# Splitting the routed tokens of an attention and expert layer into parts of five and three batches, and moving twelve row normalisations from VectorE to ScalarE

## What is computed

```python
x = _layernorm(x + attention(x))               # 8 batches x 512 tokens x 256
# experts: 16 routed ones, 4 chosen per token (gate_w), width 128; one shared expert of width 256
c[token, expert] = score of the 4 chosen experts, else 0
y = sum over experts e of  c[t, e] * (silu(x @ w1[e]) * (x @ w3[e])) @ w2[e]
z = (silu(x @ ws1) * (x @ ws3)) @ ws2
x = _layernorm(x + y + z)
```

## Time and profile before

| | |
|---|---|
| time, three runs | 698.48, 701.73, 703.09 us; median 701.73 us |
| profiled execution | 698.33 us, of it 696.5 us from the first to the last instruction (the span) |
| PE busy | 517.0 us (74%) |
| DVE busy | 427.1 us (61%) |
| ACT busy | 300.6 us (43%) |
| POOL busy | 290.6 us (42%) |
| first and last start of a pair's L1036 | 274.3 and 583.2 us |
| granted TensorE clock, mean | 0.925 |

### The profile page before, as it was taken

How to read it: one execution, slowest core, us unless ns; L and a number is a source line. 1 busy time by engine, 2 the same in 40 slices (tenths; PEclk the granted TensorE clock), 3 DMA queues, 4 the chain that set the end, 5 groups by cost and what they waited for, 6 DMA issues and landing times.

```text
span 696.5 us, 13485 instructions
## 1 busy us (share of the span) xinstructions
PE 517.0 (74%) x3554; PEld 355.2 (51%) x3555; DVE 427.1 (61%) x1200; ACT 300.6 (43%) x659; POOL 290.6 (42%) x334
## 2 busy tenths in 40 slices
PE   1899886789897787888886787888887779782300
PEld 1355543455454356676674566676765666441100
DVE  2447783777755877557654344366757657585384
ACT  2536644446334252555554555355645446121000
POOL 1000126365455421545644200634435450787664
PEclk9999999799999989999999999899999999997555
DMA  7022338285561302677767776677777763334232
GB/s 193 25 76 77 124 118 288 75 274 192 202 225 54 113 31 69 220 231 241 252 243 247 252 226 210 189 232 226 222 246 230 240 198 137 99 120 123 83 113 98
DMA packets 64091, 118.63 MB, mean 170 GB/s; under 512 B 9760, under 2 KB 23088, under 8 KB 64048
## 3 DMA queue, kind: packets, MB, share of 16 engines
q1 hardware_dynamic: 51216, 84.55, 37.2%
q0 software_dynamic: 12288, 33.57, 15.4%
q10 hardware_dynamic: 544, 0.00, 0.0%
HBM read 55.17 MB, written 62.91 MB: 170 GB/s over the span
## 4 chain that ended last, share of the span: by engine, by line
PE 35%; issue 17%; DVE 17%; SPq 8%; POOL 7%; ACT 5%; DMA 5%; another core or an unknown queue 5%; DVEq 0%; ACTq 0%; POOLq 0%
PE t L1340 4%; PE h_even L1149 3%; PE h_even L1151 3%; PE h_even L1150 3%; PE h_odd L1149 3%; PE h_odd L1151 3%; PE h_odd L1150 3%; DMA kv<-expert_in 2%; PE y L1186 2%; SPq L327 2%; POOL q_fm L452 2%; SPq L330 2%; POOL wa_stage L452 2%; POOL gate L452 2%
## 5 line engine op out<-in xcount | busy, mean ns | idle before, releaser
L440 POOL DMA_INDIRECT expert_in<-x_all,slots x128 | 132.9, 1038 | 111.7 <-PE h_odd L1151 45.1
L1340 PE MATMUL t<-ident,kv 128*128 128x128 f32 x384 | 61.7, 283 | 23.8 <-DMA kv<-expert_in 16.6
L452 POOL DMA_INDIRECT wa_stage<-expert_out,result_of x64 | 62.9, 982 | 28.2 <-issue 17.5
L452 POOL DMA_INDIRECT q_fm<-expert_out,result_of x32 | 32.1, 1003 | 89.8 <-DMA expert_out<-q_exp 64.1
L1044 DVE TENSOR_TENSOR wa_lo<-bias_heads,wa_hi 128x256 bf16<-128x256 f32 x96 | 40.5, 422 | 46.6 <-ACT wa_hi L642 37.2
L426 POOL TENSOR_SCALAR neg_mean<-mv 128x4 f32<-128x4 f32 x16 | 4.6, 290 | 148.7 <-DVE mv L699 148.5
L1340 PEld LDWEIGHTS t<-ident,kv 128*128 128x128 f32 x384 | 44.9, 145 | 33.8 <-issue 17.6
L1025 DVE TENSOR_TENSOR xsT_lo<-t,xsT_hi 128x512 bf16<-128x512 f32 x72 | 49.4, 688 | 13.2 <-ACT xsT_hi L617 6.6
L1150 PE MATMUL h_even<-xsT_lo,we_hi 128*128 128x256 bf16 x192 | 53.6, 279 | 2.2 <-issue 2.2
L1149 PE MATMUL h_even<-xsT_hi,we_hi 128*128 128x256 f16 x192 | 53.5, 279 | 1.8 <-DVE bias_heads L1036 1.3
L1151 PE MATMUL h_even<-xsT_hi,we_lo 128*128 128x256 f16 x192 | 53.6, 279 | 1.2 <-issue 1.1
(11 more groups left out here) (222 smaller groups left out, 1522.0 us busy)
## 6 DMA issues: line engine op xcount, KB each, us to landing
kv<-expert_in SPq DMA_DIRECT2D x96, 256.0 KB
expert_out<-k_exp SPq DMA_DIRECT2D x48, 256.0 KB
expert_out<-q_exp SPq DMA_DIRECT2D x48, 256.0 KB
expert_in<-wa_stage SPq DMA_DIRECT2D x16, 512.0 KB
expert_in<-wa_stage SPq DMA_DIRECT2D x32, 256.0 KB
stage<-in_L_ffn_w SPq DMA_DIRECT2D x48, 128.0 KB
x_in<-in_L_attn_x SPq DMA_DIRECT2D x8, 512.0 KB
out<-gated SPq DMA_DIRECT2D x8, 512.0 KB
```

Of the source, the lines that this page charges most:

```text
L440: pool.indirect_dma_start(xs_dram[b // WB], bass.IndirectOffsetOnAxis(ap=slots[:, b, t, j:j + 1], axis=0), x_all[:, b, t, :], None).then_i ...
L452: pool.indirect_dma_start(y_got[i][:, j, :], None, ys_dram[w], bass.IndirectOffsetOnAxis(ap=result_of[:, b, t, j:j + 1], axis=0)).then_inc ...
L1340: last = pe.transpose(t_bank[r % 2][:, c * 2 * P + i * P:c * 2 * P + (i + 1) * P], xs[r][:, i, c * P:(c + 1) * P], ident[:, :])
```

## The change

Part 0 now has five batches (0 to 4) and 56 pairs, part 1 three batches (5 to 7) and 40 pairs; there are still 96 pairs. What follows from it and what goes with it:

- `SPREAD` is 4, not 3: POOL dispatches 16 times in each of the iterations 3 to 7, 80 in all, which is all of part 0. Beside the pairs of part 0 it dispatches 48 times, not 64, a tile every 4 pairs.
- Beside the 40 pairs of part 1 POOL gathers 20 tiles (80 indirect DMAs), not 16 beside 48. Tile k waits for pair 56 + 17k/9. DVE adds 18 of the 20 tiles in the pairs 6 to 39 of the part, the last two in the first two `shared_hidden` of the tail.
- ACT, not DVE, normalises batches 0 to 2, one tile in a pair, from pair 16, 23 and 31 of the part. `rstd_of` now waits, for the layer norms behind the first of them, until the norm ahead of it has been applied (`out_ready`).
- In the tail POOL gathers 12 tiles, not 16. The two `rstd_of` for batches 3 and 4 both stand behind the four gathers of batch 5. DVE keeps its order, with a tile's number four higher at each step; the statistics of batches 5 and 6 now stand in the loop over batches, and 8 sums fewer are left.
- `count_region` for part 0 moves from batch 5 to batch 6 of the attention. One scratch area of the plan moves to `q_exp`. The loops of ACT and DVE over the pairs of part 1 are written out; those of PE and SP stay loops.

```diff
-SPREAD = 3
+SPREAD = 4
...
-    WB = NB // WAVES
-    WT = WB * TT
+    BATCHES = (5, 3)
+    START = (0, BATCHES[0], NB)
...
+    TILES = [TT * n for n in BATCHES]
+    NPAIR = [n * TOP_K // 2 + E for n in TILES]
...
+    EARLY = 3
...
+    SUM_PAIRS = (6, 40)
+    SUMMED = 18
+    NORM_PAIR = (16, 23, 31)
...
@@ rstd_of
                 pool.tensor_tensor(var_eps[:, :], mv[:, :, 1], eps[:, :], ALU.add).then_inc(rstd_step, 1)
+                if ln > NB:
+                    pool.wait_ge(out_ready, ln - NB)
...
@@ gather
-                if 0 < k < WT:
-                    pool.wait_ge(h_ready, NPAIR + (3 * k if k < WT - TT else 3 * WT - 13 + 2 * (k - WT + TT)))
+                if w == 0 and k > 0:
+                    pool.wait_ge(h_ready, FIRST[1] + 17 * k // 9)
...
@@ POOL beside the pairs of part 0
-            for i in range(WT):
+            for i in range(TILES[1]):
                 if i > 0:
-                    pool.wait_ge(h_ready, 5 * i // 2)
+                    pool.wait_ge(h_ready, 4 * i)
...
@@ POOL, gathers of both parts
-                for b in range(WB * w, WB * (w + 1)):
+                for b in range(START[w], START[w + 1]):
                     for t in range(TT):
                         gather(TT * b + t)
-                        if b > 0 and t == (1 if w == 0 else TT - 1):
+                        if w == 0 and t == TT - 2 and 0 < b <= EARLY:
                             rstd_of(NB + b - 1)
+                    if w == 1:
+                        for ln in range(EARLY if b == START[1] else b - 1, b):
+                            rstd_of(NB + ln)
...
@@ ACT
+            def final_norm(b, t):
+                if t == 0:
+                    act.wait_ge(rstd_ready, NB + b + 1)
+                    if b > 0:
+                        act.wait_ge(out_stored, 16 * b)
+                last = act.activation(o_sb[:, t, :], x_all[:, b, t, :], ACT.Identity, bias=shift[:, t:t + 1],
+                                      scale=rstd[:, t:t + 1])
...
+            norms = {NORM_PAIR[b] + t: (b, t) for b in range(EARLY) for t in range(TT)}
+            for p in range(NPAIR[1]):
+                pair(FIRST[1] + p, p % RING, PAIR_GROUPS[0] + p // RING, p < NPAIR[1] - 2, norms.get(p))
...
@@ DVE, pairs of part 1
+            for i in range(SUMMED * TOP_K):
+                at = SUM_PAIRS[0] + i * (SUM_PAIRS[1] - SUM_PAIRS[0]) // (SUMMED * TOP_K)
+                sums[at].append((i // (TT * TOP_K), i // TOP_K % TT, i % TOP_K))
...
@@ DVE, tail
-            for n in range(WB, NB):
-                at = 2 * (n - WB)
+            for n in range(EARLY, NB):
+                at = SHARED * (n - EARLY)
...
-                if n < WB + 2:
+                    if n > EARLY + 1:
+                        whole_norm(n - 2)
                     whole_stats(n - 1)
-            whole_stats(WB + 1)
```

More of the change, by code:

```diff
@@ L353, in _ @@
             sp.wait_ge(rows_ready, 1)
-            for b in range(WB):
+            for b in range(BATCHES[0]):
                 sp.wait_ge(dispatched[b], 16 * TT * TOP_K)
@@ L364, in _ @@
             sp.wait_ge(fill_rows_ready, 2)
-            with sp.Fori(3, (last - 1) // 2) as q2:
+            with sp.Fori(3, 5) as q2:
                 group(0, 2 * q2 + 1, fill=E + 2 * RING * (q2 - 3))
                 group(0, 2 * q2 + 2, fill=E + 2 * RING * (q2 - 3) + RING)
+            for q in range(11, last):
+                group(0, q)
             sp.wait_ge(rows_ready, 2)
-            for b in range(WB, NB):
+            for b in range(BATCHES[0], NB):
                 sp.wait_ge(dispatched[b], 16 * TT * TOP_K)
@@ L383, in _ @@
                 group(1, 2 * q2)
-            group(1, 5)
             store_out(0)
-            for q in range(6, 9):
+            for q in range(5, 7):
                 group(1, q)
             store_out(1)
-            for q in range(9, last):
+            for q in range(7, last1):
                 group(1, q)
             for r in range(-3, RING):
-                store_ys(1, RING * last + r, r % RING)
-            with sp.Fori(WB - 2, NB) as b:
+                store_ys(1, RING * last1 + r, r % RING)
+            with sp.Fori(EARLY - 1, NB) as b:
                 store_out(b)
@@ L625, in ys_copy, with pair @@
                                ACT.Copy).then_inc(ys_copied, 1)
-            def pair(g, r, group, ahead=True):
+            def final_norm(b, t):
[5 more added lines that the diff above has]
+                                      scale=rstd[:, t:t + 1])
+                if t == TT - 1:
+                    last.then_inc(out_ready, 1)
+            def pair(g, r, group, ahead=True, norm=None):
                 if ahead:
@@ L642, in pair, with group @@
                 act.activation(aT_hi[r % 2][:, :], a_pair, ACT.Copy).then_inc(at_hi_ready, 1)
-            def group(q, last=False):
+                if norm is not None:
+                    final_norm(*norm)
+            def group(q):
                 for r in range(RING):
-                    pair(RING * q + r, r, q, not (last and r >= 2))
-            all_groups = WAVES * GROUPS_OF_PAIRS
+                    pair(RING * q + r, r, q)
+            all_groups = ALL_GROUPS
             act.wait_ge(k_ready, NB)
@@ L1026, in xst_lo, with pair @@
                                   xsT_hi[r][:, :, :], ALU.subtract).then_inc(xst_lo_ready, 1)
-            def pair(g, r, ahead=True, add=None, norm=None, whole=True, part=None):
+            def pair(g, r, ahead=True, add=(), part=None):
                 if ahead:
@@ L1037, in pair @@
                 if add:
-                    combine(0, *add[0], whole)
-                if norm is not None:
-                    final_norm(norm, r)
+                    combine(0, *add[0])
                 if part:
@@ L1073, in final_norm, with group @@
                     last.then_inc(out_ready, 1)
-            def group(q, b=None, tiles=(), norm=None, whole=True, parts=(), last=False):
+            def group(q, parts=()):
                 for r in range(RING):
-                    add = [(b, i // TOP_K, i % TOP_K) for i in tiles[r]] if tiles else None
-                    pair(RING * q + r, r, not (last and r >= 2), add, norm, whole,
-                         parts[r] if r < len(parts) else None)
-            q1 = GROUPS_OF_PAIRS
+                    pair(RING * q + r, r, part=parts[r] if r < len(parts) else None)
+            q1 = PAIR_GROUPS[0]
             xst_lo(0, 0)
@@ L1098, in _ @@
             dve.wait_ge(shared_added, EARLY)
-            thirds = [((), (0,), (1, 2), (3, 4)), ((5,), (6,), (7, 8), (9,)), ((10,), (11, 12), (13,), (14, 15))]
-            halves = [[(8 * h + 2 * r, 8 * h + 2 * r + 1) for r in range(RING)] for h in range(2)]
-            group(q1)
-            for i in range(3):
-                group(q1 + 1 + i, 0, thirds[i])
-            with dve.Fori(1, EARLY) as b:
-                group(q1 + 1 + 3 * b, b, thirds[0])
-                group(q1 + 2 + 3 * b, b, thirds[1], norm=b - 1)
-                group(q1 + 3 + 3 * b, b, thirds[2])
-            group(q1 + 1 + 3 * EARLY, EARLY, halves[0], whole=False)
-            group(q1 + 2 + 3 * EARLY, EARLY, halves[1], norm=EARLY - 1, whole=False, last=True)
-            tiles = [(b, t) for b in range(WB, NB) for t in range(TT)]
+            sums = [[] for p in range(NPAIR[1])]
+            for i in range(SUMMED * TOP_K):
+                at = SUM_PAIRS[0] + i * (SUM_PAIRS[1] - SUM_PAIRS[0]) // (SUMMED * TOP_K)
+                sums[at].append((i // (TT * TOP_K), i // TOP_K % TT, i % TOP_K))
+            for p in range(NPAIR[1]):
+                pair(FIRST[1] + p, p % RING, p < NPAIR[1] - 2, sums[p])
+            tiles = [(0 if k < TILES[0] else 1, k // TT, k % TT) for k in range(SUMMED, NB * TT)]
             def whole_stats(b):
```

131 lines of the change are left out of this document (65 added, 66 removed).

## The result

The change made the kernel slower: 736.47 us median of 4 runs (733.41 to 738.03) against 702.08 of before, ratio 1.049, 95% interval 1.044 to 1.055. The forecast was 689 us, the range ended at 705. Later comparisons found the opposite on the same code, ratio 0.990. What differs between the two is whether TensorE's work gets through beside GpSimd's runs of indirect transfers; why it does at one time and not at another stays open.

A forecast was written before the change was run, and what follows sets the result against it. The prediction took POOL's list of gathers to bound the tail, with no engine busy throughout the pairs. Terms -18.6 + 4 + 0.5 + 0.5 + 0.5 = -13.1 us took 701.7 to 688.6 us, range 681 to 705.

The forecast's parts named there:

- The pairs: Part 1's 40 pairs, with more gathers a pair, run slower, partly offset by fewer dispatches in part 0: +4 us.
- Attention: POOL's 16 dispatches an iteration instead of 12 add 5 us of its time but mostly fit: +0.5 us.
- rival E: From the follow-up runs: the counting and filling moved into the attention are what lengthened it; no chance given.
- The tail: Behind the pairs, POOL gathers four tiles fewer, so the last group starts and the span ends earlier: -18.6 us.
- POOL's pace in part 1: 20 tiles and three norm steps, 108 us, fit into some 120 us of pairs: +0.5 us.
- The norms on ScalarE: Twelve final norms moved from DVE to ACT, 7.2 us there against 4.2 us less on DVE: +0.5 us.
- Loops written out: ACT and DVE execute fewer register instructions but fetch more code: 0 us, bounds -3 and +3.
- the gathers slow the pairs: POOL's steadier gather traffic slows all 40 pairs of part 1, costing 27.6 us: 711 us; chance 0.2.
- PE's pause comes onto the path: In the tail, PE's unexplained pause at batch 6's down product recurs and delays the end: 698.7 us; chance 0.2.

The follow-up runs named there:

- dear: Comparisons, and their traces, in which the unchanged kernel before took about 700 us (702.08, 708.24, 699.57).
- cheap: Comparisons, and their traces, in which the unchanged kernel before took about 645 us (644.27, 644.92, 643.30).
- the kernel before with pauses: Kernel before plus a 1.05 us GpSimd operation and wait behind every fourth scatter and every fourth gather of part 0's tokens: 643.12 us (0.998), again 641.92 (0.994).
- before_plain: Kernel before, word for word, run again for a second trace in which TensorE stops: 700.63 us, ratio 1.000.

## Why the prediction was wrong

- **The pairs (+4, bounds -6 and +9): the step that failed; measured +34.7.** I priced a gather by how the pace went with gathers a pair, from stretches of 12 to 27 us, and took a value between the ends. In a dear trace the cost is not one of each gather but of a run's length: four in a row cost some 1.6 us, and the next ones hold TensorE for about their full 1.25 us each. Of the three stretches the two slow ones, 4 pairs in 16 us and 2 in 12, each held a run of 8; the third, 9 pairs in 27 us, had its 16 gathers in runs of four. Averaging them hid it, and "a pair is no faster where POOL sends nothing" was true and no argument. In the cheap traces the pairs took 4.2 us less than in the kernel before with pauses.
- **Attention (+0.5, bounds 0 and +3): failed too; measured +20.6.** "5 us more of POOL's time, ending where it ended" asked whether POOL had room, which it had. That TensorE's work is held up while POOL issues wasn't among the terms. It isn't all: in the cheap traces the first pair starts at 271.3, and at 263.6 in the kernel before with pauses, 7.7 us more and beyond the bound of +3. What these are stays open; the counting and filling that were moved there (rival E) are not excluded for them.
- **The tail (-18.6): right in mechanism, measured -16.1.** The wait ahead of the second norm step was 8.15 us, forecast 6.6; from the second group's end to the third's start it was 2.9 us, forecast 2.0. Some of what was gained belonged to the hold-up: the wait of 4.82 us ahead of the last group has no like in the cheap trace of the kernel before with pauses (third group to 608.7, last from 611.0), and there the part behind the last pair gave 10.5 us.
- **POOL's pace in part 1 (+0.5)** counted whether 20 tiles fit into the pairs. They did, and that was the trouble: it didn't ask how they would be grouped. **The norms on ScalarE (+0.5)**: 0.586 us each, no cost seen, and moving them back gave nothing. **Loops written out (0)**: no run tried them alone.
- **The rival "the gathers slow the pairs" (711 us, 0.2)** had the right place and the right test, 3.75 us a pair (it became 4.3), but the wrong reason: shared DMA engines. What it took from the Trainium skill ("DMA: Bandwidth & Descriptors", Issuing engines are not separate DMA queues) isn't what costs here: with a sixteenth of the bytes the 40 pairs still took 165.5 us. Its size, 27.6 us, was too small since it took half of what the two bad stretches showed. **"PE's pause comes onto the path" (698.7, 0.2)** had the clue in hand: 15 us of TensorE standing still, called a possible accident. Laying POOL's rows beside it would have shown it inside a run of 16 transfers. It is no accident of one moment either, as a pause of like size came one batch earlier in `before_plain`. The page had a second clue, 5% of the chain on "another core or an unknown queue" in a program of one core.
- In cheap comparisons the forecast of the sum, -13 us, stands against -6 measured; against the kernel before with pauses (643.7 us span) the spans differ by -7.0: +7.7 up to the first pair, -4.2 in the pairs, -10.5 behind the last.

What stays open is what differs between dear and cheap comparisons; the same chip showed both, and every run of one comparison agreed. Open too is what holds TensorE's work up. A supply of instructions that isn't renewed was my first thought; the Trainium skill ("Runtime: NRT & Kernel Launch", Instruction fetch mechanics) says that each engine's sequencer fetches blocks ahead by a DMA queue of its own. The traces speak against it: in the changed kernel's trace no instruction transfer lies between 560 and 600 us, where two runs of 8 hold TensorE up, and matmuls already on record reach their readers 9.6 us late, which missing instructions don't explain. Every execution here comes with its span and granted clock, so each was recorded by the profiler, and no run shows whether the recording itself has a part in it.

## What to carry to other kernels

When a wait in the chain has no releaser in a program of one core, lay the rows of every other engine over it before calling it an accident, POOL's DMA issues above all. Ask also how long after its last matmul record a product is read: the record alone looks healthy for some 30 matmuls too long. Cost a move of GpSimd's indirect transfers by the length of the runs that it makes, not by their number or bytes. Single transfers, each behind a pair's gate, left part 0 at 159 us against 157 in a cheap trace; runs of four with a gap of a microsecond that a late GpSimd can't skip left part 1 at 131 us, against 172 unbroken and 113 in a cheap trace. Where TensorE isn't held up such gaps are a loss, so compare the kernel before and after there too. And set times only against those of the same comparison: the kernel before itself differed by 60 us between them, and the change's sign with it.

## What the hardware did that I had not expected

- In dear comparisons TensorE did 48 matmuls in the first 5 us of a run of 16 indirect transfers and 16 in the next 14.8 us; in cheap ones 48 and then 240 in 30.6 us, with like rows on GpSimd.
- In the dear trace a product on record at 478.43 was read at 488.02, with some 30 later matmuls on record by then; in the cheap one the same took 0.3 us.
- A pause of GpSimd of some 1.3 us, one 1.05 us operation, is enough to start TensorE afresh: 172 matmuls in 24.7 us.
- Bytes don't matter to it: with 64-byte rows and DMA engines 16% busy the matmuls thinned out just the same, 18 in 15.6 us.
- A plain transfer of 128 KB took GpSimd 0.54 us to issue, an indirect one 0.94 us and 0.30 more until the next.
